# A batched mixture-of-experts kernel: the first weight's low halves made by GpSimd in the first two batches and kept in device memory, and three parts of the tile table moved behind the seventh batch's slots

## The reference, cut to what matters

```python
u = x @ W_in + b_in                      # 256 -> 768
x0, x1, v = split(short_conv(u), 3)      # three taps along the sequence
v = v * x1
v = causal_fft_conv(v, k, filter_bias)   # k comes from a small sine network
x = layernorm(x + (v * x0) @ W_out + b_out)

probs = softmax(x @ gate_w.T)            # 16 experts, the best 4 of each token
h1, h3 = x @ w1[e].T, x @ w3[e].T        # 256 -> 128 each, for the chosen experts e
moe = sum_e weight_e * ((silu(h1) * h3) @ w2[e].T)
shared = silu(x @ sw1.T) * (x @ sw3.T) @ sw2.T
x = layernorm(x + moe + shared)
```

## Time and profile before

| | |
|---|---|
| median of three runs | 626.38 us (626.25 to 626.77) |
| profiled execution, its time | 617.06 us |
| its span (first to last instruction) | 615.2 us |
| granted TensorE clock, mean | 0.935 |
| PE, DVE, ACT, POOL busy | 527.1, 449.4, 370.5, 347.3 us |

### The profile page before, as it was taken

How to read it: one execution, slowest core, us unless ns; L and a number is a source line. 1 busy time by engine, 2 the same in 40 slices (tenths; PEclk the granted TensorE clock), 3 DMA queues, 4 the chain that set the end, 5 groups by cost and what they waited for, 6 DMA issues and landing times.

```text
span 615.2 us, 11085 instructions
## 1 busy us (share of the span) xinstructions
PE 527.1 (86%) x3184; PEld 456.8 (74%) x3184; DVE 449.4 (73%) x1053; ACT 370.5 (60%) x844; POOL 347.3 (56%) x320
## 2 busy tenths in 40 slices
PE   5997999999999989598387789898988989899762
PEld 2786878787877778476257679897978989888651
DVE  5878899999898999678597724444445778877544
ACT  4745486868685867534272436565756566776444
POOL 0332124868686886628738655555555667667630
PEclk9997999999999999987858799899999998999778
DMA  7999553988594748429935865555548999889964
GB/s 241 198 234 329 71 126 113 280 225 200 113 228 141 192 146 184 142 62 314 350 98 182 235 184 156 164 157 152 181 149 283 297 300 307 286 289 320 337 218 142
DMA packets 79006, 128.07 MB, mean 208 GB/s; under 512 B 10358, under 2 KB 57911, under 8 KB 78650
## 3 DMA queue, kind: packets, MB, share of 16 engines
q1 hardware_dynamic: 42714, 61.21, 34.9%
q0 software_dynamic: 28688, 58.35, 33.8%
q10 hardware_dynamic: 7552, 7.88, 3.6%
HBM read 75.89 MB, written 47.35 MB: 200 GB/s over the span
## 4 chain that ended last, share of the span: by engine, by line
PE 53%; DVE 20%; ACT 9%; issue 8%; another core or an unknown queue 4%; DMA 3%; SPq 2%; POOL 1%; ACTq 0%; DVEq 0%; POOLq 0%
PE bank L1034 7%; PE bank L1036 7%; PE bank L817 7%; PE bank L1035 7%; PE bank L839 5%; PE bank L871 4%; PE bank L1085 4%; PE bank L953 2%; PE bank L1057 2%; PE bank L1003 2%; PE bank L991 2%; SPq L541 1%; DVE w_lo L1610 1%; ACT ty L1318 1%
## 5 line engine op out<-in xcount | busy, mean ns | idle before, releaser
L784 POOL DMA_INDIRECT token_parts<-ty,goes x144 | 142.4, 989 | 91.4 <-issue 32.7
L755 POOL DMA_INDIRECT expert_rows<-row,slot x112 | 128.7, 1150 | 74.4 <-issue 32.0
L1034 PE MATMUL bank<-w_hi,xtT_hi 128*128 x288 | 89.9, 312 | 10.2 <-DVE xtT_lo L1783 7.7
L1035 PE MATMUL bank<-w_lo,xtT_hi 128*128 x288 | 84.2, 292 | 0.4 <-issue 0.4
L1036 PE MATMUL bank<-w_hi,xtT_lo 128*128 x288 | 83.1, 288 | 1.5 <-issue 1.5
L1034 PEld LDWEIGHTS bank<-w_hi,xtT_hi 128*128 128x128 f32 x288 | 57.1, 198 | 14.5 <-issue 14.3
L1783 DVE TENSOR_TENSOR xtT_lo<-bank,xtT_hi 128x512 fp32r<-128x512 f32 x72 | 49.5, 689 | 20.6 <-issue 14.2
L1768 DVE TENSOR_TENSOR taT_lo<-bank,taT_hi 128x256 fp32r<-128x256 f32 x72 | 30.3, 421 | 44.8 <-ACT taT_hi L1290 26.4
L1296 ACT ACTIVATE tsl<-bank 128x256 f32<-128x256 f32 x72 | 29.6, 411 | 55.0 <-PE bank L1036 29.5
L1318 ACT ACTIVATE ty<-bank,tail 128x256 f32<-128x256 f32 x144 | 62.0, 494 | 0.0
L1035 PEld LDWEIGHTS bank<-w_lo,xtT_hi 128*128 128x128 f32 x288 | 57.2, 199 | 1.8 <-issue 1.8
(11 more groups left out here) (212 smaller groups left out, 1356.2 us busy)
## 6 DMA issues: line engine op xcount, KB each, us to landing
xt<-expert_rows SPq DMA_DIRECT2D x144, 129.0 KB
row<-token_parts SPq DMA_DIRECT2D x18, 640.0 KB
xT<-in_xT SPq DMA_DIRECT2D x8, 512.0 KB
xtok<-in_b_out SPq DMA_DIRECT2D x8, 512.0 KB
xtok<-in_x POOLq DMA_DIRECT2D x8, 512.0 KB
x<-taps POOLq DMA_DIRECT2D x8, 512.0 KB
x<-ups POOLq DMA_DIRECT2D x8, 512.0 KB
w_hi<-in_w POOLq DMA_DIRECT2D x1, 4096.0 KB, 16.9
```

The lines of the kernel that those rows point to most:

```text
L755: pool.indirect_dma_start(out=rows_d, out_offset=bass.IndirectOffsetOnAxis(ap=slot[q][:, n:n + 1], axis=0), in_=src[:, n // TOPK, n % TOPK ...
L784: pool.indirect_dma_start(out=parts_d, out_offset=bass.IndirectOffsetOnAxis(ap=goes[:, q_ * UNROLL + u:q_ * UNROLL + u + 1].bitcast(U32), ...
L1034: te_.matmul(ps, x_hi, w_hi, start=first, stop=False)
L1035: te_.matmul(ps, x_hi, w_lo, start=False, stop=False)
```

## The change

- GpSimd makes the low halves of the first weight, eight subtractions of 128x1024 (`rest_w`): two in `body(0)` behind `round_x(2)`, two behind `add_newest(1)`, two in `body(1)` behind `add_x(1)`, two behind `round_x(3)`. Each waits for `w13_hi` and for a plain piece of the weight.
- SyncE loads the plain pieces (512 KB each) into four slots in the `row` tile, which the first stage does not use for rows before batch 1's end, stores each result to a new memory area `w13_rest`, and loads the next piece into the freed slot (`load_raw`, `store_rest`, placed in `body(0)` and `body(1)`).
- `load_w13` reads the finished low halves from `w13_rest`, at the same places in the program as before; the eight `low13` of VectorE are gone.
- VectorE's and ScalarE's first use of `row` waits until the eight stores have landed.
- Parts 0 to 2 of `table(0)` stand behind `slots` and `gated` in `body(7)`, ahead of `end_rows(6, 0)` and the residual; part 3 stays behind the norm's scales. The scratch of the first table moves from `xtok` to `prod`.
- `w13_hi` and `w2_hi` raise a semaphore each.

```diff
             def load_w13(n):
 
-                k = E // NPART
-                sp.dma_start(w13_lo[:, n * PART:(n + 1) * PART].bitcast(F32).rearrange("p (e c n) -> p e c n", e=k, c=DC),
-                             io["w13"][n * k:(n + 1) * k].rearrange("e (c p) n -> p e c n", p=P)).then_inc(ld_w13[n], 16)
+                for s in range(RAW):
+                    sp.wait_ge(rest_out[s], 16 * (W13 // LOW // RAW))
+                sp.dma_start(w13_lo[:, n * PART:(n + 1) * PART].bitcast(F32), rest_d[:, n * PART:(n + 1) * PART]).then_inc(ld_w13[n], 16)
+
+            def load_raw(n):
+
+                s, k = n % RAW, LOW // (DC * 2 * HID)
+                if n < RAW:
+                    sp.wait_ge(k_filt, 2)
+                else:
+                    sp.wait_ge(rest_out[s], 16 * (n // RAW))
+                sp.dma_start(raw[s].rearrange("p (e c n) -> p e c n", e=k, c=DC),
+                             io["w13"][n * k:(n + 1) * k].rearrange("e (c p) n -> p e c n", p=P)).then_inc(ld_raw[s], 16)
+
+            def store_rest(n):
+
+                sp.wait_ge(rest_made, n + 1)
+                sp.dma_start(rest_d[:, n * LOW:(n + 1) * LOW], raw[n % RAW]).then_inc(rest_out[n % RAW], 16)
...
             def body(i, q, h):
+                if is0(i):
+                    for n in range(RAW):
+                        load_raw(n)
                 if two_next(i):
                     load_xT(i + 2)
+                if is0(i):
+                    for n in range(2):
+                        store_rest(n)
+                        load_raw(n + RAW)
+                if is1(i):
+                    for n in range(RAW, 2 * RAW):
+                        store_rest(n)
...
                     sp.dma_start(xtok[:, :, :], bias).then_inc(ld_bias, 16)
+                if is0(i):
+                    for n in range(2, RAW):
+                        store_rest(n)
+                        load_raw(n + RAW)
...
+            def rest_w(n):
+
+                s, at = n % RAW, slice(n * LOW, (n + 1) * LOW)
+                pool.wait_ge(ld_moe, 16)
+                pool.wait_ge(ld_raw[s], 16 * (n // RAW + 1))
+                nc.gpsimd.tensor_tensor(out=raw[s].bitcast(F32R), in0=raw[s], in1=w13_hi[:, at].bitcast(F32),
+                                        op=ALU.subtract).then_inc(rest_made, 1)
...
                 if is1(i):
                     add_x(i)
+                    for n in range(4, 6):
+                        rest_w(n)
                 if two_next(i):
                     round_x(i + 2)
+                if is0(i) or is1(i):
+                    for n in (range(6, 8) if is1(i) else range(2)):
+                        rest_w(n)
...
                     add_newest(i + 1, 1 - q)
+                    for n in range(2, 4):
+                        rest_w(n)
...
                     slots(i, q, h, 6)
                     gated(i)
+                    dve.wait_ge(cut_made, len(CUTS))
+                    table(0, range(3))
                     end_rows(i - 1, 0)
                     residual(i)
                     norm_scales(i)
-                    dve.wait_ge(ld_moe, 32)
-                    for n in range(3):
-                        low13(n)
-                    dve.wait_ge(cut_made, len(CUTS))
-                    table(0)
+                    dve.wait_ge(ld_moe2, 16)
+                    table(0, range(3, 4))
                     end_rows(i - 1, 1)
```

More of the change, by code:

```diff
@@ L79 @@
 LOW = 1024
+RAW = 4
 GROUPS = (range(8), range(8, TT * TOPK))
@@ L152, in build @@
         rows_d = nc.dram_tensor("expert_rows", [NROWS, ROW], F32, kind="Internal").ap()
+        rest_d = nc.dram_tensor("w13_rest", [P, W13], F32, kind="Internal").ap()
         parts_d = nc.dram_tensor("token_parts", [NTOK * PARTS + NPAD, D], F32, kind="Internal").ap()
@@ L222, in build @@
         decay, filt = x1
+        raw = [early[:, n * LOW:(n + 1) * LOW] for n in range(RAW)]
         cuts = sb("cuts", [P, NCLASS, E])
         edge = sb("edge", [P, NCLASS + 1, E])
[L227 to L233, removed]
         tab_col = [sb(f"tab_col{g}", [P, 2], I32) for g in range(2)]
@@ L275, in build @@
             taps = ab_("taps", [P, DC, L])
+        table_room = (prod[:, 0, :, :].rearrange("p a n -> p (a n)"), xtok[:, :, :].rearrange("p t d -> p (t d)"))
         w13_lo = sb("w13_lo", [P, W13], F32R)
@@ L336, in build @@
         ld_w13 = [sem(f"ld_w13_{n}") for n in range(NPART)]
-        ld_w2, lo_made = sem("ld_w2"), sem("lo_made")
+        ld_w2, lo_made, ld_moe2, rest_made = (sem(n) for n in ("ld_w2", "lo_made", "ld_moe2", "rest_made"))
+        ld_raw = [sem(f"ld_raw{n}") for n in range(RAW)]
+        rest_out = [sem(f"rest_out{n}") for n in range(RAW)]
         res_out = [sem(f"res_out{u}") for u in range(UNROLL)]
@@ L703, in body @@
                     pool.dma_start(w2_hi[:, :].rearrange("p (e d) -> p e d", e=E),
-                                   io["w2"].rearrange("e h d -> h e d")).then_inc(ld_moe, 16)
+                                   io["w2"].rearrange("e h d -> h e d")).then_inc(ld_moe2, 16)
                 third = not (is0(i) or is1(i))
@@ L1023, in _ @@
             batches(pe_e, body)
-            pe_e.wait_ge(ld_moe, 32)
+            pe_e.wait_ge(ld_moe, 16)
+            pe_e.wait_ge(ld_moe2, 16)
             pe_e.wait_ge(tab_ready, 32)
@@ L1064, in turn @@
                         pe_e.wait_ge(act_silu, B)
-                        pe_e.wait_ge(lo_made, W13 // LOW)
+                        for n in range(NPART):
+                            pe_e.wait_ge(ld_w13[n], 16)
                     pe_e.wait_ge(t_xlo, k + 1)
@@ L1093, in turn @@
                         pe_e.wait_ge(dve_acc, 2 * B)
-                        pe_e.wait_ge(lo_made, (W13 + W2) // LOW)
+                        pe_e.wait_ge(lo_made, W2 // LOW)
                     pe_e.wait_ge(t_alo, k + 1)
@@ L1275, in fill_rows @@
             def fill_rows(i, q, ts=range(TT)):
+                if is0(i):
+                    for s in range(RAW):
+                        act.wait_ge(rest_out[s], 16 * (W13 // LOW // RAW))
                 for t in ts:
@@ L1581, in body @@
                     logits(i, 4)
-                    low13(3)
                     top(i)
                     add_shared(i - 1, 1 - q, h - 1 if q == 0 else h)
-                    low13(4)
                     slots(i, q, h, 5)
@@ L1590, in body @@
                         end_rows(i - 1, half)
-                    for n in range(5, W13 // LOW):
-                        low13(n)
                     return
@@ L1603, in body @@
                     end_rows(i - 1, 0)
-            def low13(n):
-                if n % (PART // LOW) == 0:
-                    dve.wait_ge(ld_w13[n // (PART // LOW)], 16)
-                at = slice(n * LOW, (n + 1) * LOW)
-                ve.tensor_tensor(w13_lo[:, at], w13_lo[:, at].bitcast(F32), w13_hi[:, at].bitcast(F32),
-                                 ALU.subtract).then_inc(lo_made, 1)
             def low2(n):
@@ L1705, in end_rows @@
                 at = slice(half * TT // 2, (half + 1) * TT // 2)
+                if is0(i):
+                    for s in range(RAW):
+                        dve.wait_ge(rest_out[s], 16 * (W13 // LOW // RAW))
                 if row_of(i) is row:
@@ L1716, in table @@
             def table(g, parts=range(4)):
+                temp = table_room[g]
+                cnt = temp[:, 0:SEG].rearrange("p (k e) -> p k e", e=E)
+                cend = temp[:, SEG:2 * SEG]
+                past = temp[:, 2 * SEG:4 * SEG].rearrange("p (a n) -> p a n", a=2)
+                move = temp[:, 4 * SEG:5 * SEG]
+                cnt_i = temp[:, 5 * SEG:6 * SEG].rearrange("p (k e) -> p k e", e=E).bitcast(I32)
+                tab_f = temp[:, 6 * SEG:6 * SEG + 2]
                 for part in parts:
```

## The result

| | before | after |
|---|---|---|
| median of seven runs | 626.25 us (613.85 to 628.17) | 637.03 us (627.37 to 640.71) |
| profiled execution, its time | 617.06 us | 627.37 us |
| its span | 615.2 us | 625.6 us |

The ratio, which compares only the faster executions of each kernel, is 1.0215 (1.0133 to 1.0296): the change makes the kernel slower, by 10.8 us in the medians and by 10.3 us in the two profiled executions. The forecast was 636.5 us.

The account below looks back on a forecast made before the run. TensorE holds 53% of the chain of waits, VectorE 20%; VectorE has no slack where GpSimd gets work. Stops of 14.8 us less 4.7 saved give +10.1: 626.38 to 636.5 us, range 620.5 to 643.

Parts of the forecast that it names:

- Pieces 0 and 1: First batches, beside VectorE's taps and make_z: 4.0 us lost, with w13_hi landing at 54.
- Pieces 2 and 3: First two batches, from 64.4 to 69.8 against products beginning at 68.51: 1.3 us lost, 5.4 at most.
- Pieces 4 to 7: Behind add_x from 76.0 and round_x(3), beside two-input VectorE work: 9.5 us lost, one or two instructions slipping in between.
- The stores cost nothing: SyncE's queue and first use of row: no cost, up to 2 us if the pieces are late.
- the rival without stops: First two batches: GpSimd's pieces yield or fall in VectorE's gaps; 621.7 us, down to 617.6; chance 0.20.
- The passage, -4.7 us: Between the stages: three pieces at the end of body(8) save 3.4 us, the clock 1.3; bounds -2.6 and -8.8.
- the tile loads were not last: At the passage: tile loads can start some 6 us before 318.52, but bring 0 of their own.
- if that cover goes: Moved table parts stick out by 0.8 us, hidden by a 4.05 us wait; without that wait they cost 0.8.
- The clock term: TensorE's first 12 expert matmuls may take half of 2.56 us without the idle time: -1.3 us, bounds 0 and -1.3.
- wash: First two batches: GpSimd waits for VectorE's gaps, each piece costs about 0.6 us; 626.4 us; chance 0.07.
- The late landing: w13_hi lands past 60 us behind the plain loads, later pieces fall deeper in the products; 639.6 us; chance 0.05.

Follow-up runs that it names:

- with four extra ones: The kernel before with four extra GpSimd subtractions of 128x1024 in the second batch, no transfers, VectorE's pieces kept; 571.63 us, ratio 1.0133.
- The run with writes only: The changed kernel with each of GpSimd's eight subtractions replaced by two fills with zero, transfers and waits kept; 564.54 us, ratio 1.0029.
- the three pieces alone: The kernel before without VectorE's last three low-half pieces in body(8), nothing else changed; 561.01 us, ratio 0.9976.
- the table alone: The kernel before with only the moved tile table and its prod scratch, VectorE making all eight pieces; 562.82 us, ratio 0.9994.
- the run with the table put back: The changed kernel with the tile table back in one piece behind the norm's scales, GpSimd's eight pieces and transfers kept; 572.78 us, ratio 1.0167.
- with four pieces: The changed kernel with only four pieces by GpSimd, at places where VectorE reads matmul banks, VectorE making the other four; 573.98 us, ratio 1.0197.

## Why the prediction was right, step by step

**The mechanism held.** Two-input VectorE instructions stop while GpSimd subtracts; it gave 15.2 us where the sum had 14.8. Two of its terms were wrong and cancelled.

- *Pieces 0 and 1, 4.0 us: cost nothing.* `w13_hi` landed at 56.6, not 54. Of the 5.8 us against before, 4.3 are a later issue (38.16 for 33.91): beside the four plain loads GpSimd waited 6.07 us for a tap's transfer, where it was 1.69. The last tap was running when the first piece began at 56.70; this tap and `make_z` behind it (57.25) took their usual time, and it was the piece that was held, 4.06 us for 2.35. For this the forecast had no row.

  The Trainium skill, SBUF — State Buffer, "Who interferes with whom", says that issue order decides which of the two blocks. The recorded starts do not bear that out: `make_z` began 0.55 us behind the piece and was let through, and the three products that were stopped for the length of two or four pieces began 0.42 and 0.34 us (here) and 0.24 us (with four extra ones) ahead of GpSimd's subtraction. Each of the three ended 1.1 us behind the last piece, with 1.22 us of its own to do, so it had hardly begun when it was stopped. GpSimd's times are the roughest of the profile; what decides at distances of half a microsecond stays open.
- *Pieces 2 and 3, 1.3 us: cost 5.5.* The step read the start of the products (68.51) and the end of the pieces (69.8) from the trace of before. With pieces 0 and 1 ahead of them and a later landing, pieces 2 and 3 began at 68.92 instead of 64.4, 0.4 us into the first product, and held it through both.
- *Pieces 4 to 7, 9.5 us: cost 9.7.* "One or two instructions slip in between" was wrong for pieces 4 and 5 (one stop of 6.60 us), and right for 6 and 7 only because these waited for their reloads, 1.64 and 2.64 us. Pieces 4 and 5 also began at 81.57 and not 76.0. `add_x` ahead of them waits for the bias, and SyncE issued that at 71.75, not 64.40, because two stores and two reloads stood ahead of it; the prediction had the queue free there. It cost nothing, VectorE being 5.5 us late itself.
- *The stores cost nothing*: true of this kernel, since VectorE was late. The run with writes only shows 3.4 us at the third `yx` once VectorE is on time, in part for that reason. Had the rival without stops come true, its 621.7 us would have left these out.

**The passage, -4.7 us.** The step that failed is "the tile loads were not last": the three pieces alone bring 1.4 us and the table alone 0.4, neither clear of no change, since each is what is late next for the other. With both gone, the quick chip shows 326.46 - 305.92 = 20.5 us from the last residual to the first product in the changed kernel, against 314.22 - 291.15 = 23.1 with the table alone: 2.5 us sooner. The moved table was not needed for it: in the run with the table put back it is 20.7, because the three pieces ahead of the table are gone as well. In the changed kernel the moved parts only cost. From the eighth `yx` to the last residual it is 305.92 - 298.21 = 7.7 us with them and 304.40 - 297.89 = 6.5 without; the prediction had 0.8 for this "if that cover goes", and took 0.

The clock term was right in sign and nearly in size there: the first twelve expert products begin within 1.40 us, against 2.51 with the table alone, 1.1 us less where 1.3 was forecast. On the slow chip nothing came of it: 2.51 us before and after. Windows of 5 us from the first product on, of the kernel with the table alone and then of the changed kernel, both on the quick chip:

```profile
314.00:319.00 5.00, 4.78 (x19) 4.44 (x20) 2.72 (x4) 0.38 (x1) 3.78 (x5) 0.56 0.29 98
```

```profile
326.00:331.00 5.00, 4.54 (x32) 4.29 (x33) 2.84 (x5) 1.32 (x5) 3.85 (x4) 1.00 0.81 246
```

32 matmuls at a clock of 1.00 against 19 at 0.56. But both gains are lent. The changed kernel there, SyncE's pads, then TensorE at the second group's first tile:

```profile
334.96 12.28 SPq L555 DMA_DIRECT2D expert_rows<-in_c_pad  x16
```

```profile
352.77 1.08 PE L1130 MATMUL bank<-ident,xt 128*128 128x128 f32 x4 [4.76 <-DMA xt<-expert_rows]
```

and ScalarE, the seventh and the eighth `tsl` activation (one per tile of products), in the changed kernel and then in the one with the table alone:

```profile
348.04 0.38 ACT L1344 ACTIVATE tsl<-bank 128x256 f32<-128x256 f32 x1 [0.45 <-PE bank L1080]
...
358.15 0.38 ACT L1344 ACTIVATE tsl<-bank 128x256 f32<-128x256 f32 x1 [1.79 <-PE bank L1080]
```

```profile
340.34 0.39 ACT L1290 ACTIVATE tsl<-bank 128x256 f32<-128x256 f32 x1 [0.44 <-PE bank L1030]
...
343.87 0.39 ACT L1290 ACTIVATE tsl<-bank 128x256 f32<-128x256 f32 x1 [0.65 <-PE bank L1030]
```

Counted from each kernel's last residual, the changed one is at 348.04 - 305.92 = 42.1 us where the other is at 340.34 - 291.15 = 49.2, 7 us ahead; one tile later it is at 52.2 against 52.7. The second group's tile loads, which SyncE issues behind 12 us of pads, take the lead back. Counted from the last residual to the end of the span, 0.6 us is left in this pair of traces (268.5 against 269.1); by the early loss and the medians (15.0 - 12.1, next paragraph) it is 3. The kernels with writes only and with four pieces keep some 4 us (265.1 and 264.8); why they do was not traced.

**Late results.** On the slow chip TensorE's results reach the waiting engines late in both traces, at places that differ. The kernel is 15.2 us late at the second `yx` and 15.8 at the sixth (236.5 against 220.7), but 9.2 at the eighth (301.3 against 292.1): before, the first half of the seventh `yx` waited 4.79 us and its second half for a result that was 6.7 us late, which has no counterpart after; where the rest was regained I have not traced. At the last residual it is 5.9 us late, because the 4.05 us of the earlier trace rows are gone too; the passage then loses 2.8 by its own late result. That the profiled difference comes out at +10.3 against the +10.1 of the sum, with a late passage in place of the sooner one, is luck in its parts. On the quick chip the sum reads plainly, against the kernel with the table alone: 15.0 us late at the eighth `yx` (298.2 against 283.2), 12.3 at the first product (326.46 against 314.22), and 12.1 in the medians against the kernel before: the early loss as forecast, and 3 us of passage where 4.7 were.

**The rivals.** Not stopped and wash fall with the four stretched instructions. The late landing did happen, by 2.6 us and not by 6, and missed its own condition; pieces 2 and 3 did fall wholly inside the products, as it says.

## What to carry to other kernels

Before giving an engine with room some more work, list the instructions of its neighbour that have both inputs in on-chip memory in that stretch, and count every such place as a stop of the whole run of back-to-back work, not of one piece; move only what fits where there are none. Work handed over by way of memory also brings stores that the buffer's next user waits for. And where two short stalls end close to each other, time them removed one by one and both together, and follow the gain to the next transfer before counting it.

## What the hardware showed

- A two-input VectorE instruction, once stopped, stays stopped over GpSimd subtractions that follow one another, and over the issue of a transfer between them: 11.93 us for an instruction of 1.22, over four. A wait and a fill of 0.95 us between them, together, let it in (2.90, 2.85 and 3.32 us).
- GpSimd is held in its turn: 4.06 us for a subtraction of 2.35 that began beside the last tap and 0.55 us ahead of `make_z`.
- A VectorE instruction that is recorded as started 0.24 to 0.42 us ahead of GpSimd's subtraction can still be the one that is stopped (11.93, 6.60 and 6.75 us for 1.22).
- GpSimd's fills stopped nothing here: products of 1.22 us beside fills of 0.96 and 1.46 us.
- The kernel before takes 563 us at the quick level and 620 to 626 at the slow one, with VectorE and GpSimd instructions of the same length. At the slow one TensorE's results are seen late: from the end of a TensorE instruction to the arrival of its semaphore, the delays of more than 1 us add up to about 280 us over the trace of before (they overlap; the longest is 10.8). In the trace of the kernel with the table alone, at the quick level, there is at most one. The ends of matmuls are modelled in the profile, so whether the result or only its signal is late is not shown, and why stays open.
